# A recurrence with a gated feed-forward layer on one core: the order of TensorE's products within a round

## What is computed

```python
xk = x * mix_k + xx * (1 - mix_k)          # the same for xv and xr
k = xk @ Wk.T;  v = xv @ Wv.T;  sr = sigmoid(xr @ Wr.T)

w = -exp(time_decay)                        # one value per channel; u = time_first
aa, bb, pp = 0, 0, -1e38
for t in range(4096):
    q  = max(pp, u + k[t])
    y[t] = (exp(pp - q) * aa + exp(u + k[t] - q) * v[t]) / (exp(pp - q) * bb + exp(u + k[t] - q))
    q2 = max(pp + w, k[t])
    aa = exp(pp + w - q2) * aa + exp(k[t] - q2) * v[t]
    bb = exp(pp + w - q2) * bb + exp(k[t] - q2)
    pp = q2

x = layernorm(x + (sr * y) @ Wo.T)
h = silu(x @ Wg.T / 127) * (x @ Wu.T / 127) # 768 hidden channels, integer weights
x = layernorm(x + h @ Wd.T / 127)
```

## Time and profile before

| | |
|---|---|
| time, median of three runs | 332.47 us |
| time of the profiled execution | 333.66 us |
| its span in the profile | 331.9 us |
| mean granted TensorE clock | 0.946 of full |
| TensorE busy (matmul) | 285.6 us, 86% |
| VectorE busy | 296.6 us, 89% |
| ScalarE busy | 216.1 us, 65% |
| GpSimd busy | 157.3 us, 47% |
| chain that ended last: VectorE, TensorE, issue, ScalarE | 37%, 30%, 16%, 13% |

### The profile page before, as it was taken

The page is one execution under the profiler, slowest core; times in us unless marked ns, Lnnn a source line. Parts: engine busy times, 40 slices in busy tenths (PEclk is TensorE's granted clock), DMA queues, the critical chain, the costliest instruction groups (busy, mean ns, idle before and its releaser), DMA issues.

```text
span 331.9 us, 4559 instructions
## 1 busy us (share of the span) xinstructions
PE 285.6 (86%) x1250; PEld 208.3 (63%) x1250; DVE 296.6 (89%) x522; ACT 216.1 (65%) x411; POOL 157.3 (47%) x125
## 2 busy tenths in 40 slices
PE   8576889999499986999689995999879995999892
PEld 6333766467365875568665784658655684868782
DVE  5999897999969997999989999699989999589764
ACT  3579646696709874388908876198735877099365
POOL 2557485029930499007960299205990088006030
PEclk9999799999879995999979998799979999799999
DMA  7703000300030010401012010400103010101002
GB/s 266 272 0 127 3 1 4 127 18 15 5 101 25 1 65 4 128 0 49 15 51 76 0 63 0 127 0 0 63 0 95 0 65 2 34 1 63 3 4 97
DMA packets 13527, 16.32 MB, mean 49 GB/s; under 512 B 704, under 2 KB 11200, under 8 KB 13504
## 3 DMA queue, kind: packets, MB, share of 16 engines
q1 hardware_dynamic: 12816, 15.48, 14.3%
q10 hardware_dynamic: 688, 0.53, 0.5%
HBM read 11.81 MB, written 4.19 MB: 48 GB/s over the span
## 4 chain that ended last, share of the span: by engine, by line
DVE 37%; PE 30%; issue 16%; ACT 13%; DVEq 1%; ACTq 0%
PE bank_b L992 12%; DVE hid L761 5%; DVE rwkv L708 5%; PE bank_b L1024 5%; PE bank_a L1024 4%; DVE wts L637 3%; DVE pmax L620 3%; ACT L515 3%; DVE state L666 3%; ACT den L454 3%; DVE state L654 3%; DVE den L674 2%; DVE gap L627 2%; PE bank_a L982 2%; DVE kv L660 2%
## 5 line engine op out<-in xcount | busy, mean ns | idle before, releaser
L344 POOL TENSOR_TENSOR hlo<-hid,hhi 128x512 fp32r<-128x512 f32 (+1 forms) x36 | 49.2, 1367 | 143.1 <-ACT hhi L498 143.1
L329 POOL TENSOR_TENSOR mix<-mix,xt 128x512 f32<-128x512 f32 (+1 forms) x46 | 55.5, 1238 | 13.9 <-ACT mix L424 13.9
L1047 PE MATMUL bank_a<-wd_r,hhi 128*128 128x256 f32 x192 | 49.1, 294 | 11.3 <-DVE hlo L769 11.3
L992 PE MATMUL bank_b<-woT,rwkv 128*128 128x256 f32 x128 | 41.6, 495 | 13.9 <-DVE rwkv L708 11.1
L1047 PE MATMUL bank_a<-wd_r,hlo 128*128 128x256 f32 x192 | 46.9, 282 | 0.0
L1047 PEld LDWEIGHTS bank_a<-wd_r,hhi 128*128 128x128 f32 x192 | 36.4, 190 | 15.8 <-issue 14.9
L992 PEld LDWEIGHTS bank_b<-woT,rwkv 128*128 128x128 f32 x128 | 32.0, 256 | 22.4 <-issue 12.4
L474 ACT ACTIVATE lnv<-mv,eps 128x4 f32<-128x4 f32 (+1 forms) x18 | 5.2, 289 | 59.7 <-DVE mv L720 59.7
L498 ACT ACTIVATE hhi<-hid 128x512 fp32r<-128x512 f32 (+1 forms) x54 | 31.1, 578 | 16.9 <-DVE hid L761 16.9
L1047 PEld LDWEIGHTS bank_a<-wd_r,hlo 128*128 128x128 f32 x192 | 36.5, 190 | 0.3 <-issue 0.2
L416 ACT ACTIVATE wts<-wts 128x512 f32<-128x512 f32 (+1 forms) x54 | 27.9, 579 | 8.5 <-DVE wts L637 8.5
(11 more groups left out here) (105 smaller groups left out, 591.8 us busy)
## 6 DMA issues: line engine op xcount, KB each, us to landing
xt<-xT SPq DMA_DIRECT2D x7, 513.0 KB, 3.7
xrow<-x SPq DMA_DIRECT2D x7, 512.0 KB, 4.0
out<-y SPq DMA_DIRECT2D x6, 512.0 KB, 2.8
wg_i<-wg SPq DMA_DIRECT2D x1, 768.0 KB, 8.4
wu_i<-wu SPq DMA_DIRECT2D x1, 768.0 KB, 9.9
wd_i<-wd SPq DMA_DIRECT2D x1, 768.0 KB, 11.6
out<-y SPq DMA_DIRECT2D x3, 256.0 KB, 2.1
xt<-xT SPq DMA_DIRECT2D x2, 257.0 KB, 2.9
```

The costliest lines, as they stand in the source:

```text
L329: nc.gpsimd.tensor_tensor(mix[:, i, h, 0:n], mix[:, i, h, 0:n], xt[:, h, 0:n], ALU.add).then_inc(mixed, share(c, i, h))
L344: nc.gpsimd.tensor_tensor(hlo[:, m, 0:n], hid[:, m % NH, 0:n], hhi[:, m, 0:n].bitcast(f32), ALU.subtract).then_inc(hlo_ready, 1)
L992: mm = nc.tensor.matmul(attn[:, q, :], rwkv[:, h, q * P:(q + 1) * P], woT[:, h, :], start=(h == 0), stop=(h == CH - 1))
L1047: mm = nc.tensor.matmul(ffn[:, q, :], hp.bitcast(f32) if full else hp, w[:, m, :], start=(m == 0 and q % 2 == 0 and part is hhi), stop=(m ...
```

## The change

The change has four parts. TensorE's list: from round 2 on the V product of the next chunk stands before `attention_out` instead of behind K, and in rounds 2 to 6 the first half of R stands before the transposes and the second behind them, as round 1 already had it. The mixing order: from chunk 3 on V, K, R instead of K, V, R, for ScalarE and GpSimd, with a function `place` that gives the counts. VectorE's list, in rounds 1 to 7: `shift_rows1` stands before the first running maximum instead of behind it, the gap and the three arguments of half 0 follow directly on its running maximum, and the low parts of x1 stand before and behind the second gap.

```diff
+        def place(c, i):
+
+            return i if isinstance(c, int) and c < 3 else (1, 0, 2)[i]
+
...
             def mixing(c, i, h):
-                pool.wait_ge(dx_scaled, (c - 1) * (3 * CH) + (i * CH + h + 1))
+                pool.wait_ge(dx_scaled, (c - 1) * (3 * CH) + (place(c, i) * CH + h + 1))
...
                 if nxt:
-                    mix_chunk(j + 1, (K, R) if isinstance(j, int) and j == 1 else range(3))
+                    mix_chunk(j + 1, (K, R) if isinstance(j, int) and j == 1 else (V, K, R))
...
                 if nxt:
-                    scale_chunk(j + 1, (K, R) if isinstance(j, int) and j == 1 else range(3))
+                    scale_chunk(j + 1, (K, R) if isinstance(j, int) and j == 1 else (V, K, R))
...
                 mean_var(j, stats1, mv1, mv1_ready)
                 mean_var(j - 1, stats2, mv2, mv2_ready)
+                shift_rows1(j)
                 running_max(j + 1, 0)
-                shift_rows1(j)
+                gaps(j + 1, 0)
+                exp_args(j + 1, 0)
                 running_max(j + 1, 1)
-                gaps(j + 1, 0)
+                shift_rows2(j - 1)
+                x1_low(j, 0)
                 gaps(j + 1, 1)
-                exp_args(j + 1, 0)
-                shift_rows2(j - 1)
-                exp_args(j + 1, 1, (IN_NEW, IN_OLD))
-                x1_low(j, 0)
                 x1_low(j, 1)
-                exp_args(j + 1, 1, [OUT])
+                exp_args(j + 1, 1)
...
-                    pe.wait_ge(mixed, (c - 1) * (3 * CH) + (i + 1) * CH)
+                    pe.wait_ge(mixed, (c - 1) * (3 * CH) + (place(c, i) + 1) * CH)
...
+                if nxt and not (isinstance(j, int) and j < 2):
+                    project(j + 1, V)
                 if not last(j):
                     attention_out(j)
                 if nxt and not first(j):
                     project(j + 1, K)
-                    if not (isinstance(j, int) and j == 1):
-                        project(j + 1, V)
                 if first(j) or last(j + 1):
                     project(j + 1, R)
-                if isinstance(j, int) and j == 1:
+                elif nxt:
                     project(j + 1, R, [0])
...
                 if nxt and not first(j) and not last(j + 1):
-                    project(j + 1, R, [1] if isinstance(j, int) and j == 1 else range(CH))
+                    project(j + 1, R, [1])
```

## The result

The changed kernel takes 352.68 us, the median of four runs (351.17 to 353.35), against 332.35 us for the kernel before. The ratio is 1.0618, interval 1.0576 to 1.0661: slower by 6%. The forecast was 345 us, range 337 to 352: it had the sign, and most of the mechanism. The profiled execution took 353.35 us (span 351.5), 19.7 us more than the profiled one of before, where the sum had 12.4.

A forecast was written before the change was run, and what follows sets the result against it. VectorE's wait for the output product bounds: a lap is D (a round's first `divide`) to that product's end plus 29.1 us. 333.66 + (0.6 + 2.9 + 2.7 + 5.1 + 1.1 = 12.4) - 1.2 gives 345 us, range 337 to 352.

The forecast's parts named there:

- The constant: From the output product's end to the next round's first `divide`: VectorE's list, to stay at about 29.1 us.
- the two small terms of VectorE's order and GpSimd's earlier low part: Rounds 2 to 6: VectorE's order costs 0.6 us a round, an earlier low part shortening VectorE's scan gives 0.6 back.
- the granted clock is 1.00 through the output products: Sign against the prediction: full 2.4 GHz clock during the output products, where half of the slow-clock extra was expected to stay.
- I take half of the mean extra of these three rounds (1.67, 3.32, 1.97; mean 2.3), 1.2 us: Rounds 4 to 6, output product: 1.2 us of slow clock stays a round, bounds 0 and 3.3; rounds together +5.1 us.
- I take the middle: Rounds 2 and 3: V starts midway between mixed and the output product's old start; +2.9 and +2.7 us.
- rival A: V fills no pause, so all of V adds to the chain: 19.9 us, median 352; chance 0.22.
- Nor do the new waits cost: Behind the output product, `gate_up` waiting for the second gap and later low parts of x1 cost nothing; otherwise 0.6 us a round.
- So this earns nothing directly: TensorE's list behind the output product, 3.43 us shorter ahead of `gate_up`, gains no time directly.
- +1.1: Round 7: V, half as long, costs 0.7 us and one more gap ahead of x1's low part 0.4 us.
- B: Clock stays at 2.4 GHz and V starts as soon as mixed: 332.5 us, not slower; chance 0.11.
- C: TensorE is the bound, so V in the pause brings its whole list forward: -9 us, 323.5; chance 0.05.
- It priced VectorE's order and R's halves at about nothing: Rounds 2 to 6: these parts sum to 0, bounds -0.6 and +0.6 us a round; round 1 alone pays 0.6.

The follow-up runs named there:

- Experiment 8: The changed kernel with the mixing back in the old order K, V, R: 364.06 us, 1.0995 to the kernel before.
- Experiment 5: The changed kernel with matmuls on zeros in TensorE's two pauses of rounds 2 to 7, six ahead of the last eight of `down`, four behind: 343.03 us, 1.0329.
- experiment 6: The changed kernel with six matmuls on zeros ahead of the last eight of `down` and one behind them, rounds 2 to 7: 341.13 us, 1.0250.
- experiment 10: The kernel before with six matmuls on zeros ahead of the last eight of `down` and three behind them, rounds 2 to 7: 321.49 us, 0.9672.
- experiment 7: The changed kernel with matmuls on zeros in round 7 only, ahead of the transposes and of `gate_up`: 351.82 us, 1.0632.
- experiment 1: The changed kernel with V put back behind K and mixing K, V, R; VectorE's new order and R's halves kept: 345.95 us, 1.0428.
- experiment 3: The kernel before with VectorE's new order alone: 339.10 us, 1.0229.
- experiment 4: The kernel before with R's halves around the transposes alone: 338.22 us, 1.0217.
- experiment 12: The kernel before with six and three matmuls on zeros, and R's halves moved behind `gate_up`'s first and second hidden tile in rounds 3 to 7: 333.87 us, 1.0038.
- experiment 2: The kernel before with only V moved ahead of the output product and mixed first: 348.76 us, 1.0474.

## Why the prediction was wrong in size

**What held.** The lap is "D to the end of the output product" plus a constant; V put 3.43 us into the first part, and no part of TensorE's shorter list behind it came back. The constant, 29.1 forecast, was 28.98 to 29.09 in rounds 2 to 5 (in round 6, with the half chunk behind it, 28.23, before 28.24), the two small terms of VectorE's order and GpSimd's earlier low part cancelled, round 1 cost 0.5 us (0.6 forecast), V was mixed at D + 2.7 and started at D + 2.85 (2.80). Experiment 8 moves V's mixing and the lap follows. One of the signs that the prediction named against itself did come, "the granted clock is 1.00 through the output products": the slow part was in V, where it had not been looked for.

**The step that failed first: "I take half of the mean extra of these three rounds (1.67, 3.32, 1.97; mean 2.3), 1.2 us".** The forecast counted 1.1 us of the mean 2.3 as given back by the shorter pause; 0.35 came back. V was slow in every round: 5.38, 5.39 and 5.41 us from its start to that of the output product in rounds 4 to 6, 1.95 to 1.98 more than at the full clock, and 2.9 us more in round 2. Rounds 4 to 6 came to +8.0 instead of +5.1. Of the 2.9 us, 2.3 are the clock; the rest is that an output product at the full clock was counted from start to start (3.43), and its end was measured from its last record (3.62). Experiment 5 shows that it is the clock and its cause the pauses: filled, V takes 3.43. The forecast looked at the pause that the change shortens; in rounds 2 and 4 to 6 the clock fell one pause earlier, inside `down`, which the change doesn't shorten. So the mis-sized term is what the clock gives back, and not what it costs: the slow clock costs both kernels about the same (experiments 6 and 10).

**Second: "I take the middle" for rounds 2 and 3.** V started at D + 4.20 and D + 4.15, where the output product had started (D + 3.77 and D + 4.22), and the profile names issue as the cause. Its mixing was done by D + 2.8, and the chain puts 1.47 and 1.41 us of issue between the two. It was about the bound of rival A, not the middle: +7.5 instead of +5.6. The rows to go by were the starts of the output product there, 0.5 and 0.95 us behind the end of rwkv, where it took 0.14 in rounds 4 to 6. The start is not fixed, though: the same list gave D + 3.69 in round 2 of experiment 7.

**Third: "Nor do the new waits cost", and of the shorter list "So this earns nothing directly".** True in rounds 2 to 6, where VectorE comes to the first hidden product late. In round 7 the forecast named `gate_up` as being on the path and did not draw the consequence: TensorE with less to do there paused twice and was at the half clock for the first 6 us of `gate_up`. +4.5 instead of +1.1: 2.4 us of it are this clock and 0.5 VectorE's order (experiments 6 and 7), and 1.5 are the output product's later end, D + 11.05 instead of D + 9.52, where the forecast had 0.7; V started at D + 3.94, and the forecast's middle was D + 3.1.

These three make 2.9 + 1.9 + 3.4 = 8.2 us; the start of the program was 0.8 us shorter in the profiled execution. Together they are the 7.3 us between 12.4 and 19.7.

**The rivals.** A's number (352) was almost exact, its reason half right: in rounds 2 and 3 V filled no pause, in 4 to 6 it did, and the clock fell as often all the same. B (the clock stays up) did not happen; forced, it gives 341 and not 332.5. Of the gap 3.1 us are the output product's end in rounds 2 and 3, D + 11.2 instead of D + 9.66, 1.0 its end at D + 10.0 in rounds 4 to 6, and 2.6 round 7, where B had -2.0 and +0.6 came out. C is out: the list behind the output product is 3.43 us shorter, and the stretch behind it did not shrink by more than 0.2 us.

**What the forecast got right for the wrong reason.** It priced VectorE's order and R's halves at about nothing. With V moved that is so. Experiments 1, 3 and 4 show that both are losses by themselves, of 0.7 and 1.05 us a lap and 2.45 together: of the lists tried, they fit only the one in which V is gone from behind the output product.

## What to carry to other kernels

Before moving work into an engine's pause, ask who waits for what stands behind the pause: a pause ahead of the one product that the bounding engine waits for is not free room, and work of 3.4 us that starts 0.6 us ahead of that product's old start costs the other 2.8 (rounds 4 to 6 of experiment 6 against experiment 10: 2.8 to 2.9 us a lap). When a tuned list shows a matmul engine returning from pauses at half clock on the bounding stretch, try to fill the pause with work that needs no input and ends before the real work is ready; here that was worth 3%. And price a moved step in every round on its own, the written-out first and last ones too, since 5.3 of the 8.2 us of this miss came from rounds 2, 3 and 7, which differ from rounds 4 to 6.

## What the runs showed of the hardware

- TensorE fell to the 1.2 GHz level in every one of rounds 2 to 7 of both kernels. In rounds 4 to 6 the pauses around the fall were 1.71 and 2.00 us in the kernel before and 0.4 to 0.6, 1.71 and 0.58 us in the changed one; after six matmuls on zeros in the first pause and two in the second it stayed at 2.4 GHz through all of them. The Trainium skill, "TensorE: Matmul & The Clock Gate", section "Why this matters for your kernels", asks only for no long single idle gap; by that rule these pauses should have cost nothing. The traces disagree: several short pauses close together are enough.
- The first output or V product behind the branch in rounds 2 and 7, which are written out, and in round 3, the first turn of the loop, started up to 2.75 us behind the last matmul in the branch, put down to issue; from the second turn of the loop on V started 0.6 us behind it. With a longer program (experiment 12) one such start waited 3.81 us.
- Some of VectorE's operations on inputs in SBUF were longer beside GpSimd's: the second scan of aa took 1.67, 1.79 or 2.31 us by where GpSimd's first low part fell, and the second half of `divide` 1.6 us beside GpSimd's mixing. What starts first seems to matter. In round 4 of the kernel before the low part began 0.07 us ahead of the scan and the scan took 2.31 us; in round 3 of experiment 2 it began 0.13 us behind it, the scan took 1.27 us, and the first two low parts took 3.49 us together. The two sums of the denominator took 2.6 us, or 3.5 where GpSimd's low part began with them (experiments 2 and 12).
